# A two-layer graph network on one core: the stages between the layers reordered over four engines, and two waits of GpSimd moved

## The chip, the core and the metric

The kernel runs on one core of a Trainium2 chip. The metric is the device time of one execution in microseconds. The core has TensorE (PE, matrix products), VectorE (DVE), ScalarE (ACT), GpSimd (POOL, which here issues the indirect DMAs) and the queue of SyncE (SP), which issues the plain DMAs. Each engine works off its own queue in order and waits on semaphores.

## What is computed

6250 nodes with 128 features each, and 106250 directed edges sorted by target. Two layers, each with a layer norm and relu ahead of it and a residual behind it:

```python
h = maximum(layernorm(x), 0)
# layer 0: softmax aggregation, one weight for each edge and feature
msg = h[src] + edge_attr
m = segment_max(msg * beta, dst)
e = exp(msg * beta - m[dst])
agg = segment_sum(msg * e / segment_sum(e, dst)[dst], dst)
x = x + (agg @ H + bias + h)
h = maximum(layernorm(x), 0)
# layer 1: attention with 4 heads of 32
Wx = h @ W.T
e = leaky_relu(Wx[src] . a1 + Wx[dst] . a2, 0.2)
ex = exp(e - segment_max(e, dst)[dst])
x = x + elu(segment_sum(ex * Wx[src], dst) / segment_sum(ex, dst))
```

Everything is float32.

## The kernel before

**Groups.** In each layer the edges go by in 208 groups of 512 (NG), four blocks of 128. GpSimd fetches the source rows of a block with one indirect DMA (gather0, L658, into the ring ring_h of four groups; gather1, L689, into msg, a ring of eight). Ahead of a group it waits until its slot of the ring is free: in layer 0 until the group four back is lifted, in layer 1 until the products of the group eight back are made. Between the gathers of a group stands one more wait. In layer 0, ahead of the second gather, it is for the maxima of the group six back, turned back (unturned); in layer 1, ahead of the third, for the targets of the group four back.

**One group of layer 0.** ScalarE lifts the gathered rows into PSUM (lift0, L817), VectorE adds them to the edge's features (add0, L1141), TensorE turns the messages so that edges run along the free axis (turn0, L1395, semaphore msgT), VectorE scans them twice for the maxima of each target (maxima0, L1118 and L1123), TensorE turns the differences back (unturn0, L1401 and L1405), ScalarE makes the weights (weigh0, L799 and L803), VectorE the products (products0, L1153), TensorE sums both into a window of 512 targets with a one-hot matrix (segment_sums, L1386), and ScalarE merges the window into the accumulator acc (merge, L775 to L783). The stages of different groups overlap with fixed lags. Layer 1 does the like with narrow logits: the targets' logits (targets1, L1486), scans of 4 rows, unturn1 (L1504 and L1506), products1 (L1284).

**Between the layers** the 6250 nodes go by in 13 batches of 512 (NBAT; the last has 106). For each batch, in order:
- log0 and seed0 on ScalarE (L822, L827) make the reciprocal of the denominator from the accumulator; batch b can start when merge 196 + b is done.
- near0 on GpSimd multiplies it with both accumulators (L672 into nears(b), L674).
- lift_near0 on ScalarE copies nears(b) into PSUM (L836), quotient0 on VectorE corrects the quotient with it (L1177).
- layer_out on TensorE (L1438 the bias, L1443 the product). Its weights are every fourth column of the quotients, a step of 16 bytes.
- finish0 on VectorE adds the residual (L1183) and takes statistics (L969).

Only when all 13 are finished do the means follow (L1207, L1208), and then, again batch by batch, above1 on VectorE (subtract the mean and relu, L1216), turn_h (L1454), a copy out of PSUM (ScalarE L889 or VectorE L1242), layer_in (L1465) and the scaled copy of four tiles by ScalarE into msg (wx1, L899). The reciprocals of the spreads are made in between on VectorE by spreads1, 16 small operations (L1221 to L1231). SyncE stores each batch (L537, L539) to wx_dram, and gather1 waits for all of the stores.

The order on each engine is that of its program: ScalarE's tail of layer 0 interleaves weigh0, merge0, log0, seed0 and lift_near0 by hand; so does VectorE's with quotient0 and products0.

## Time and profile before

| | us |
|---|---|
| median of three runs (2255.95 to 2258.19) | 2258.1 |
| the profiled execution | 2257.1 |
| its span in the trace | 2255.3 |
| first gather of layer 0, from the start of the span | 37.96 |
| first gather of layer 1 | 1162.82 |

Times in the rows are microseconds from the start of the span, unless they are marked ns or stand in a column of mean ns. A row of the timeline gives the start, the duration, the engine, the line and what it writes and reads; equal neighbours are merged (x8), and the bracket tells how long the engine had stood idle before it and what ended that. "issue" is time in which an engine waited for nothing that the profile shows. PEld is TensorE's loading of weights, which runs beside its products.

### The profile page before, as it was taken

The page shows a single profiled execution, that of the slowest core. Times are in us where ns is not written, and L with a number is a line of the kernel's source. Part 1 is how long each engine was busy: PE and PEld are TensorE (multiplying, and loading weights), DVE is VectorE, ACT ScalarE, POOL GpSimd, SP SyncE. Part 2 cuts the span into 40 slices and gives each one's busy share as a digit, 9 for nine tenths or more (in the row PEclk, how much of TensorE's full clock was granted, in tenths as well). Part 3 has the DMA queues.
Part 4 walks back from the last instruction along what each step waited for, and adds up shares of the span by engine and source line. Part 5 has one row for each costly group of instructions (what it writes and reads, how often), then busy time and mean ns, then how long its engine had stood idle before and what let it go on. Part 6 is the DMA issues. An engine that isn't in the chain of part 4 may idle for free.

```text
span 2255.3 us, 62207 instructions
## 1 busy us (share of the span) xinstructions
PE 1935.5 (86%) x14541; PEld 1707.6 (76%) x14542; DVE 1986.2 (88%) x3873; ACT 1419.2 (63%) x3494; POOL 1645.6 (73%) x1739
## 2 busy tenths in 40 slices
PE   2888888888888888888969998989999999999996
PEld 1677777776776777777758888888888888888885
DVE  7999999999999999999759988888888888888886
ACT  3677777777677777777635555555555555555556
POOL 5777777777777777777627777777777777777775
PEclk9999999999999999999778999999999999999999
DMA  6444444444444444444023333333333333333331
GB/s 213 124 130 133 136 132 132 127 132 132 132 137 126 129 134 135 133 129 120 8 82 62 60 59 58 58 59 59 59 58 59 59 59 58 59 59 59 58 60 68
DMA packets 318697, 213.52 MB, mean 95 GB/s; under 512 B 169938, under 2 KB 279074, under 8 KB 318642
## 3 DMA queue, kind: packets, MB, share of 16 engines
q0 software_dynamic: 53184, 112.31, 20.9%
q1 hardware_dynamic: 264608, 100.15, 17.2%
q8 instruction: 23, 0.38, 0.1%
q10 hardware_dynamic: 850, 0.43, 0.1%
q14 instruction: 32, 0.26, 0.0%
HBM read 200.69 MB, written 10.29 MB: 94 GB/s over the span
## 4 chain that ended last, share of the span: by engine, by line
POOL 38%; issue 22%; DVE 13%; DMA 11%; PE 9%; ACT 3%; POOLq 1%; SPq 1%; DVEq 0%; ACTq 0%
POOL msg L689 25%; POOL ring_h L658 12%; DMA ring_h<-h_dram,meta_g 8%; DVE seg_max L1123 3%; DMA msg<-wx_dram,meta_g 3%; DVE sums L1118 2%; ACT banks L817 2%; PE sums L1405 2%; PE sums L1401 2%; DVE banks L1118 2%; DVE msg L1141 1%; PE banks L1395 1%; PE sums L1386 1%; PE sums L1443 1%; DVE onehot L1102 1%
## 5 line engine op out<-in xcount | busy, mean ns | idle before, releaser
L689 POOL DMA_INDIRECT msg<-wx_dram,meta_g x831 | 792.6, 954 | 299.1 <-issue 246.2
L658 POOL DMA_INDIRECT ring_h<-h_dram,meta_g x831 | 786.7, 947 | 266.2 <-issue 227.2
L1386 PE MATMUL sums<-onehot,prod 128*128 128x128 f32 x3296 | 685.7, 291 | 18.4 <-issue 6.5
L1386 PE MATMUL sums<-onehot,wgt 128*128 128x128 f32 x3296 | 669.0, 286 | 0.0
L1386 PEld LDWEIGHTS sums<-onehot,prod 128*128 128x128 f32 x3296 | 529.3, 202 | 52.7 <-issue 51.9
L1386 PEld LDWEIGHTS sums<-onehot,wgt 128*128 128x128 f32 x3296 | 532.1, 203 | 0.0
L783 ACT ACTIVATE acc<-sums 128x1022 f32 x410 | 419.9, 1024 | 0.1
L817 ACT ACTIVATE banks<-ring_h,sign 128x512 f32<-128x512 f32 x208 | 143.9, 692 | 269.9 <-DMA ring_h<-h_dram,meta_g 262.6
L1405 PEld LDWEIGHTS sums<-neg_ident,seg_max 128*128 128x128 f32 x1664 | 219.3, 192 | 100.0 <-issue 99.5
L1395 PE MATMUL banks<-ident,msg 128*128 128x128 f32 x832 | 136.7, 287 | 160.9 <-DVE msg L1141 160.9
L1118 DVE TENSOR_TENSOR_SCAN sums<-flags,seg_max,banks 4x512 f32<-4x512 bf16 x207 | 264.1, 1276 | 4.9 <-PE banks L1495 3.5
L1118 DVE TENSOR_TENSOR_SCAN banks<-flags,seg_max,banks 128x512 f32<-128x512 bf16 x207 | 264.8, 1279 | 0.0
L1123 DVE TENSOR_TENSOR_SCAN seg_max<-flags,banks 128x512 f32<-128x512 bf16 x208 | 253.9, 1220 | 7.2
L1123 DVE TENSOR_TENSOR_SCAN seg_max<-flags,sums 4x512 f32<-4x512 bf16 x208 | 251.2, 1208 | 7.2
L1395 PEld LDWEIGHTS banks<-ident,msg 128*128 128x128 f32 x832 | 88.3, 142 | 199.3 <-issue 183.5
L775 ACT ACTIVATE carried<-acc,scale 128x2 f32 x414 | 121.3, 293 | 164.2 <-PE sums L1386 147.2
L1486 PEld LDWEIGHTS banks<-window,onehotT 128*128 128x128 f32 x1664 | 213.7, 201 | 10.1 <-issue 8.9
L1405 PE MATMUL sums<-neg_ident,seg_max 128*128 128x128 f32 x1664 | 220.0, 275 | 0.0
L1141 DVE SCALAR_TENSOR_TENSOR msg<-msg,sign,banks 128x512 f32<-128x512 f32 x208 | 155.3, 746 | 72.1 <-ACT banks L817 66.7
L1401 PE MATMUL sums<-msg,ident 128*128 128x512 f32 x416 | 214.1, 597 | 2.3 <-ACT sums L803 2.2
L1486 PE MATMUL banks<-window,onehotT 128*128 128x4 f32 x1664 | 207.5, 248 | 9.1 <-DMA window<-wx_dram 8.7
L908 ACT ACTIVATE sums<-logit_d 128x16 f32<-128x16 f32 x208 | 39.1, 188 | 266.0 <-DVE logit_d L1276 263.2
(215 smaller groups left out, 2877.8 us busy)
## 6 DMA issues: line engine op xcount, KB each, us to landing
msg<-in_edge_attr SPq DMA_DIRECT2D x207, 256.0 KB, 3.2
flags<-flag_dram SPq DMA_DIRECT2D x52, 512.2 KB, 3.8
window<-wx_dram SPq DMA_DIRECT2D x832, 2.0 KB
ring_h<-h_dram,meta_g POOLq DMA_INDIRECT x831
msg<-wx_dram,meta_g POOLq DMA_INDIRECT x831
wx_dram<-msg SPq DMA_DIRECT2D x13, 272.0 KB, 2.1
nodes<-in_x SPq DMA_DIRECT2D x6, 512.0 KB, 7.1
h_dram<-acc SPq DMA_DIRECT2D x12, 256.0 KB
```

What stands on the lines that cost most here:

```text
L658: pool.indirect_dma_start(hg[0:n, s % HRING, b, :], None, h_dram, bass.IndirectOffsetOnAxis(ap=meta_g[0:n, s, b:b + 1], axis=0)).then_inc( ...
L689: pool.indirect_dma_start(msg[0:n, s, b, :], None, wx_dram, bass.IndirectOffsetOnAxis(ap=meta_g[0:n, s, b:b + 1], axis=0)).then_inc(L1["ga ...
L783: act.activation(acc[:, :, bass.ds(node + 1, WIN - 1)], where[:, :, 1:WIN], ACT.Copy).then_inc(k["merged"], 1)
L817: act.activation(row_psum, ring_h[:, s % HRING, :], ACT.Copy, scale=sign[:, 0:1]).then_inc(L0["lifted"], 1)
L1118: dve.tensor_tensor_scan(run, flag[:, 0:GE], data, before, ALU.add, ALU.max).then_inc(k["scanned"], 1)
L1123: dve.tensor_tensor_scan(seg_max[0:n, par, ::-1], flag[:, GE:0:-1], run[:, ::-1], -BIG, ALU.add, ALU.max).then_inc(k["scanned"], 1)
L1141: dve.scalar_tensor_tensor(msg[:, s, :, 0:D], msg[:, s, :, 0:D], sign[:, 0:1], row_psum.rearrange("p (b d) -> p b d", b=GB), ALU.mult, ALU.add
L1386: ins = pe.matmul(where[:, j, bass.ds(off, P)], what[:, slot, b, :], onehot[:, s, b, :], start=(b == 0), stop=(b == GB - 1), skip_group_ch ...
L1395: ins = pe.transpose(bank[s % 2][:, b * P:(b + 1) * P], msg[:, s, b, 0:D], ident[:, :])
L1401: pe.matmul(shift_psum.rearrange("p (b d) -> p b d", b=GB), ident[:, :], msg[:, s, :, 0:D], start=True, stop=False, skip_group_check=True)
L1405: ins = pe.matmul(shift_psum[:, b * P:(b + 1) * P], seg_max[:, s % 2, b * P:(b + 1) * P], neg_ident[:, :], start=False, stop=(b == GB - 1) ...
L1486: ins = pe.matmul(bank[1][:, b * H:(b + 1) * H], onehotT[:, s % 2, b * P:(b + 1) * P], window[:, s, b, :], start=True, stop=True)
```

## The change

**Waits of GpSimd in the layers.** In gather0, ahead of a group's second gather, the wait is now for the messages turned two groups back (msgT), from group 2 on. In gather1 it is ahead of the second gather, for the maxima turned back four groups back (unturned).

**End of layer 0.** lift_near0 leaves ScalarE. For batches 0 to 5 (LIFTS) TensorE does it as a product with the identity; from batch 6 on quotient0 reads nears(b) in SBUF. near0 has eight places (NEARS), four of them in ring_h. quotient0 writes its result tile by tile into msg (quot), reading its inputs with a step of four numbers, and layer_out's weights lie in one piece. layer_out(0) stands ahead of the last segment sums.

**Three parts.** Means are made for batches 0 to 5 once batch 5 is finished, for 6 to 9 behind batch 9, and for the rest at the end; the spreads of 0 to 5 behind batch 7, all others at the end. Subtracting the mean (less_mean) is now one operation for each batch, on GpSimd for eleven batches and on VectorE for 10 and 12, and the relu moves into the copy behind turn_h, on ScalarE except for batches 8 and 10. From layer_out(8) on TensorE puts turn_h and layer_in of the first batches in between. From batch 6 on VectorE scales the fourth tile (last_wx1). The stores of wx_dram are unrolled and wait for both engines.

The diff, cut to its core:

```diff
+        NEARS = 8
+        LIFTS = 6
+        EARLY = 6
+        MIDDLE = 10
+        QUOT = 4
+
         def nears(b):
-            return (diff[:, b % 2, :], hn_row[:, b % 2, :])[b // 2 % 2]
+            if b % NEARS < 4:
+                return (diff[:, b % 2, :], hn_row[:, b % 2, :])[b // 2 % 2]
+            return ring_h[:, b % 4, :]
...
-        HT_ACT = (0, 3, 6, 9, 12)
-        HT_DVE = tuple(b for b in range(NBAT) if b not in HT_ACT)
+        HT_DVE = (8, 10)
+        HT_ACT = tuple(b for b in range(NBAT) if b not in HT_DVE)
+        ABOVE_DVE = (10, 12)
+        ABOVE_POOL = tuple(b for b in range(NBAT) if b not in ABOVE_DVE)
+
+        def turn_bank(b):
+            if b < EARLY:
+                return (sums[:, 0, 0, :], bank[3])[b % 2]
+            return bank[b % 2]
 
         def wx_psum(b, t):
+            if b < EARLY:
+                return sums[:, 0, 1, 0:TW] if t == IN_BANK else bank[2][:, t * TW:(t + 1) * TW]
             return sums[:, b % 2, 1, 0:TW] if t == IN_BANK else bank[2 + b % 2][:, t * TW:(t + 1) * TW]
+
+        def tiles_of(b):
+            return range(1 if b == NBAT - 1 else GB)
+
+        def wx_by_dve(b, t):
+            return b >= EARLY and t == IN_BANK
+
+        WX_DVE = tuple(b for b in range(EARLY, NBAT - 1))
+
+        def wait_wx(eng, b):
+            eng.wait_ge(mid_wx, b + 1)
+            if b in WX_DVE:
+                eng.wait_ge(mid_wx_dve, WX_DVE.index(b) + 1)
 
         def wait_turned(eng, b):
             if b in HT_ACT:
                 eng.wait_ge(mid_hT_act, HT_ACT.index(b) + 1)
             else:
                 eng.wait_ge(mid_hT_dve, HT_DVE.index(b) + 1)
+
+        def less_mean(eng, b, done):
+            t = len(tiles_of(b))
+            lo = b * GB
+            eng.tensor_tensor(logs(b)[:, 0:t * D].rearrange("p (t d) -> p t d", d=D), nodes[:, lo:lo + t, :],
+                              norm[:, 1, lo:lo + t].rearrange("p (t a) -> p t a", a=1).to_broadcast([P, t, D]), ALU.add
+                              ).then_inc(done, 1)
...
-                    if b == 1 and later(g, 6):
-                        pool.wait_ge(L0["unturned"], g - 5)
+                    if b == 1 and later(g, 2):
+                        pool.wait_ge(L0["msgT"], g - 1)
...
-                if b >= 4:
-                    pool.wait_ge(mid_lifted, b - 3)
+                if b >= NEARS:
+                    pool.wait_ge(mid_lifted, b - NEARS + 1)
+                elif b >= 4:
+                    pool.wait_ge(L0["lifted"], NG - HRING + b % 4 + 1)
...
+            for b in ABOVE_POOL:
+                pool.wait_ge(mid_mean, 1 if b < EARLY else 2 if b < MIDDLE else 3)
+                less_mean(pool, b, mid_h_pool)
...
-                    if b == 2 and later(g, 4):
-                        pool.wait_ge(L1["targets"], g - 3)
+                    if b == 1 and later(g, 4):
+                        pool.wait_ge(L1["unturned"], g - 3)
...
-            def lift_near0(b):
-                w = LAST if b == NBAT - 1 else GE
-                act.wait_ge(mid_near, b + 1)
-                if b < 2:
-                    act.wait_ge(L0["scanned"], 2 * (NG - 1 + b))
-                else:
-                    act.wait_ge(mid_agg, b - 1)
-                act.activation(near_bank(b)[:, 0:w], nears(b)[:, 0:w], ACT.Copy).then_inc(mid_lifted, 1)
...
-                act.activation(hT[:, b % 2, 0:w], bank[b % 2][:, 0:w], ACT.Copy).then_inc(mid_hT_act, 1)
+                act.activation(hT[:, b % 2, 0:w], turn_bank(b)[:, 0:w], ACT.Relu).then_inc(mid_hT_act, 1)
...
-                if b == 0:
-                    act.wait_ge(normed, 3)
+                act.wait_ge(normed, 3 if b < EARLY else 4)
                 if b >= WXB:
                     act.wait_ge(wx_stored[b % WXB], 16 * (b // WXB))
-                for t in range(1 if b == NBAT - 1 else GB):
-                    n = b * GB + t
-                    ins = act.activation(msg[:, b % WXB, t, :], wx_psum(b, t), ACT.Copy, scale=norm[:, 0, n:n + 1])
+                for t in tiles_of(b):
+                    if not wx_by_dve(b, t):
+                        n = b * GB + t
+                        ins = act.activation(msg[:, b % WXB, t, :], wx_psum(b, t), ACT.Copy, scale=norm[:, 0, n:n + 1])
                 ins.then_inc(mid_wx, 1)
...
             def quotient0(b):
-                w = LAST if b == NBAT - 1 else GE
                 dve.wait_ge(mid_quot, b + 1)
-                dve.wait_ge(mid_lifted, b + 1)
-                rows = logs(b)[:, 0:w]
-                dve.scalar_tensor_tensor(rows, near_bank(b)[:, 0:w], 2.0, rows, ALU.subtract, ALU.mult).then_inc(mid_agg, 1)
+                if b < LIFTS:
+                    dve.wait_ge(mid_lifted, b + 1)
+                near = by_tile(near_bank(b) if b < LIFTS else nears(b), b)
+                dve.scalar_tensor_tensor(quot(b), near, 2.0, by_tile(logs(b), b), ALU.subtract, ALU.mult).then_inc(mid_agg, 1)
...
+            for b in range(NBAT):
+                if b + 1 < NBAT:
+                    quotient0(b + 1)
+                finish0(b)
+                if b == EARLY - 1:
+                    dve.wait_ge(measured, NBAT + EARLY)
+                    means(0, EARLY * GB)
+                if b == EARLY + 1:
+                    spreads(0, EARLY * GB)
+                if b == MIDDLE - 1:
+                    dve.wait_ge(measured, NBAT + MIDDLE)
+                    means(EARLY * GB, MIDDLE * GB)
+            dve.wait_ge(measured, 2 * NBAT)
+            means(MIDDLE * GB, NT)
+            dve.wait_ge(mid_mean, 3)
+
             def turned1(b):
...
+            less_mean(dve, 10, mid_h_dve)
+            less_mean(dve, 12, mid_h_dve)
+            spreads(EARLY * GB, NT)
+            last_wx1(6)
+            turned1(8)
+            last_wx1(7)
+            last_wx1(8)
+            turned1(10)
+            last_wx1(9)
+            last_wx1(10)
+            last_wx1(11)
+            dve.wait_ge(mid_wx_psum, NBAT)
...
+            def lift_near0(b):
+                pe.wait_ge(mid_near, b + 1)
+                if b < 2:
+                    pe.wait_ge(L0["scanned"], 2 * (NG - 1 + b))
+                else:
+                    pe.wait_ge(mid_agg, b - 1)
+                pe.matmul(near_bank(b), ident[:, :], nears(b), start=True, stop=True).then_inc(mid_lifted, 1)
...
-                    part = logs(b)[:, 0:LAST] if last else logs(b)[:, i:GE:GB]
-                    ins = pe.matmul(where[:, i * D:(i + 1) * D], part, phm_neg[:, :], start=False, stop=(i == t - 1),
+                    ins = pe.matmul(where[:, i * D:(i + 1) * D], quot(b)[:, i, :], phm_neg[:, :], start=False, stop=(i == t - 1),
...
+            last(unturn0, 1)
+            lift_near0(0)
+            pe.wait_ge(L0["onehots"], NG)
+            pe.wait_ge(L0["added"], NG)
+            last(sums0, 3, where=spare_sums0, free=1)
+            last(unturn0, 0)
+            lift_near0(1)
+            last(sums0, 2, free=1)
+            lift_near0(2)
+            last(sums0, 1, where=spare_sums0, free=1)
+            pe.wait_ge(phm_turned, 1)
+            pe.wait_ge(bias_split, 1)
+            pe.wait_ge(L0["weighed"], NG)
+            pe.wait_ge(L0["multiplied"], NG)
+            layer_out(0)
+            last(sums0, 0, free=1)
+            AHEAD_OUT = 8
+            for b in range(1, NBAT):
+                if b + 2 < LIFTS:
+                    lift_near0(b + 2)
+                layer_out(b)
+                if b >= AHEAD_OUT:
+                    if b == AHEAD_OUT:
+                        pe.wait_ge(L0["merged"], NG)
+                    turn_h(b - AHEAD_OUT)
+                    if b > AHEAD_OUT:
+                        layer_in(b - AHEAD_OUT - 1)
+            for b in range(NBAT - AHEAD_OUT, NBAT):
+                turn_h(b)
+                layer_in(b - 1)
+            layer_in(NBAT - 1)
             pe.wait_ge(mid_wx, NBAT)
 
 

```

## Rows read from the trace of the kernel before

**Rows 1.** The page, chain of waits that ended last, shares of the span by engine
```profile
POOL 38%; issue 22%; DVE 13%; DMA 11%; PE 9%; ACT 3%; POOLq 1%; SPq 1%; DVEq 0%; ACTq 0%
```

**Rows 2.** Waits of GpSimd, 200 to 1000 and 1200 to 2200: total, times, longest
```profile
POOL ring_h L658 <- issue: 174.7, 573, 0.3
...
POOL msg L689 <- issue: 235.8, 773, 0.3
```

**Rows 3.** Timeline, start of layer 0, GpSimd's first and tenth gather, TensorE's first turn
```profile
37.96 1.19 POOL L658 DMA_INDIRECT ring_h<-h_dram,meta_g  x1 [13.05 <-DMA h_dram<-acc]
...
49.81 0.95 POOL L658 DMA_INDIRECT ring_h<-h_dram,meta_g  x1 [0.30 <-issue]
...
54.23 1.09 PE L1395 MATMUL banks<-ident,msg 128*128 128x128 f32 x4 [2.64 <-DVE msg L1141]
```

**Rows 4.** Timeline: last gather of layer 0, a lift and the last merge, first gather after
```profile
1076.90 0.89 POOL L658 DMA_INDIRECT ring_h<-h_dram,meta_g  x1 [0.30 <-issue]
...
1094.25 0.62 ACT L836 ACTIVATE banks<-diff 128x512 f32<-128x512 f32 x1
...
1102.32 1.03 ACT L783 ACTIVATE acc<-sums 128x1022 f32 x1
...
1162.82 1.04 POOL L689 DMA_INDIRECT msg<-wx_dram,meta_g  x1 [45.95 <-DMA wx_dram<-msg]
```

**Rows 5.** Timeline, VectorE's residuals of batches 0, 1, 7 and 12
```profile
1102.86 0.69 DVE L1183 TENSOR_TENSOR nodes<-nodes,sums 128x512 f32<-128x512 f32 x1 [7.16 <-PE sums L1443]
...
1105.24 0.69 DVE L1183 TENSOR_TENSOR nodes<-nodes,sums 128x512 f32<-128x512 f32 x1
...
1121.02 0.69 DVE L1183 TENSOR_TENSOR nodes<-nodes,sums 128x512 f32<-128x512 f32 x1 [0.45 <-PE sums L1443]
...
1133.39 0.27 DVE L1183 TENSOR_TENSOR nodes<-nodes,sums 106x128 f32<-106x128 f32 x1
```

**Rows 6.** Timeline: two of the spreads' operations, first and last scaled copy by ScalarE
```profile
1136.17 0.24 DVE L1221 TENSOR_TENSOR newton<-stats 128x49 f32<-128x49 f32 x1
...
1136.45 0.21 DVE L1222 SCALAR_TENSOR_TENSOR norm<-newton 128x49 f32<-128x49 f32 x1
...
1140.18 0.91 ACT L899 ACTIVATE msg<-banks,norm 128x136 f32<-128x136 f32 x3 [2.90 <-DVE norm L1231]
...
1157.90 0.44 ACT L899 ACTIVATE msg<-banks,norm 128x136 f32<-128x136 f32 x1
```

**Rows 7.** Stretches: length, busy PE, PEld, DVE, ACT, POOL (count), clock, DMA, GB/s
```profile
1097.00:1133.00 36.00, 35.52 (x127) 27.86 (x127) 24.30 (x69) 13.74 (x30) 15.36 (x15) 0.61 0.00 1
1133.00:1159.00 26.00, 20.71 (x151) 18.81 (x151) 22.08 (x92) 16.10 (x54) 0.00 (x0) 0.89 0.31 119
```

**Rows 8.** Timeline near the end of layer 0: a turn, a second gather two groups later
```profile
1018.53 0.65 PE L1395 MATMUL banks<-ident,msg 128*128 128x128 f32 x4 [1.37 <-DVE msg L1141]
...
1020.60 0.95 POOL L658 DMA_INDIRECT ring_h<-h_dram,meta_g  x1 [0.31 <-issue]
```

**Rows 9.** TensorE: low-clock products; page row; layer_out's bias; weight loads, min/median/max ns
```profile
62.17 1.78 PE L1405 MATMUL sums<-neg_ident,seg_max 128*128 128x128 f32 x8
...
L1401 PE MATMUL sums<-msg,ident 128*128 128x512 f32 x416 | 214.1, 597 | 2.3 <-ACT sums L803 2.2
...
L1438 PE MATMUL sums<-bias_rows,ones_rows 3*128 3x512 bf16 x12 | 6.5, 543 | 0.1
...
L1443 PEld LDWEIGHTS sums<-phm_neg,elu_e x16: 309/329/332, 1105.6 to 1109.6; 128*128 128x128 f32 x16
...
L1465 PEld LDWEIGHTS banks<-w_aug,hT x74: 186/190/337, 1137.3 to 1157.2; 128*128 128x128 f32 x74
```

**Rows 10.** Timeline, layer 1: maxima of group 3 turned back, second gather of group 7
```profile
1195.74 0.39 PE L1506 MATMUL banks<-ident,seg_max 4*128 4x4 f32 x4
...
1199.19 0.94 POOL L689 DMA_INDIRECT msg<-wx_dram,meta_g  x1 [0.30 <-issue]
```

**Rows 11.** Timeline before layer 0: a sum on GpSimd, a VectorE operation beside it
```profile
22.11 1.26 POOL L636 TENSOR_TENSOR nodes<-nodes,acc 128x512 f32<-128x512 f32 x1 [0.27 <-ACT acc L738]
...
22.58 0.85 DVE L979 TENSOR_TENSOR newton<-stats 128x25 f32<-128x25 f32 x1
```

More of the change, by code:

```diff
@@ L875, in _ @@
             log0(12)
-            lift_near0(5)
             seed0(11)
             seed0(12)
-            for b in range(6, NBAT):
-                lift_near0(b)
             def turned1(b):
@@ L1199, in _, with means, spreads @@
             dve.wait_ge(pool_sum, len(POOL_SUMS))
-            for b in range(NBAT):
-                if b + 1 < NBAT:
-                    quotient0(b + 1)
-                finish0(b)
-            dve.wait_ge(measured, 2 * NBAT)
-            one, two = stats[:, :, 0:3], stats[:, :, 3:6]
-            link(dve.tensor_tensor(mean_2[:, :], one[:, :, 1], two[:, :, 1], ALU.add))
-            dve.tensor_scalar(norm[:, 1, :], mean_2[:, :], -0.5, None, ALU.mult).then_inc(mid_mean, 1)
-            dve.wait_ge(mid_mean, 1)
-            def above1(b):
-                if b >= 2:
-                    dve.wait_ge(mid_hT_psum, b - 1)
-                for t in range(1 if b == NBAT - 1 else GB):
-                    n = b * GB + t
-                    ins = dve.tensor_scalar(hn[:, b % 2, t, :], nodes[:, n, :], norm[:, 1, n:n + 1], 0.0, ALU.add, ALU.max)
-                ins.then_inc(mid_h, 1)
-            def spreads1():
-                y, t, v = norm[:, 0, :], newton[:, :], spread_v[:, :]
-                link(dve.tensor_tensor(t, one[:, :, 1], two[:, :, 1], ALU.subtract))
+            one, two = stats[:, :, 0:3], stats[:, :, 3:6]
+            def means(lo, hi):
+                link(dve.tensor_tensor(mean_2[:, lo:hi], one[:, lo:hi, 1], two[:, lo:hi, 1], ALU.add))
+                dve.tensor_scalar(norm[:, 1, lo:hi], mean_2[:, lo:hi], -0.5, None, ALU.mult).then_inc(mid_mean, 1)
+            def spreads(lo, hi):
+                y, t, v = norm[:, 0, lo:hi], newton[:, lo:hi], spread_v[:, lo:hi]
+                link(dve.tensor_tensor(t, one[:, lo:hi, 1], two[:, lo:hi, 1], ALU.subtract))
                 link(dve.scalar_tensor_tensor(y, t, 0.25, t, ALU.mult, ALU.mult))
-                link(dve.tensor_tensor(v, one[:, :, 2], two[:, :, 2], ALU.add))
+                link(dve.tensor_tensor(v, one[:, lo:hi, 2], two[:, lo:hi, 2], ALU.add))
                 link(dve.scalar_tensor_tensor(v, v, 1.0 / D, y, ALU.mult, ALU.add))
@@ L1234, in spreads1, with last_wx1 @@
                 ins.then_inc(normed, 1)
+            for b in range(NBAT):
+                if b + 1 < NBAT:
[12 more added lines that the diff above has]
+            dve.wait_ge(mid_mean, 3)
             def turned1(b):
[L1237 to L1238 removed]
                 dve.wait_ge(mid_hT_psum, b + 1)
[L1240 to L1250 removed]
+                dve.wait_ge(mid_wx_psum, b - 1)
+                dve.tensor_scalar(hT[:, b % 2, :], turn_bank(b), 0.0, None, ALU.max).then_inc(mid_hT_dve, 1)
+            def last_wx1(b):
+                dve.wait_ge(mid_wx_psum, b + 1)
+                if b == WX_DVE[0]:
+                    dve.wait_ge(normed, 4)
+                dve.wait_ge(wx_stored[b % WXB], 16 * (b // WXB))
+                n = b * GB + IN_BANK
+                dve.tensor_scalar(msg[:, b % WXB, IN_BANK, :], wx_psum(b, IN_BANK), norm[:, 0, n:n + 1], None, ALU.mult
+                                  ).then_inc(mid_wx_dve, 1)
+            less_mean(dve, 10, mid_h_dve)
[10 more added lines that the diff above has]
+            dve.wait_ge(mid_wx_psum, NBAT)
             def one_hot1(g, s, use):
@@ L1412, in _ @@
             pe.wait_ge(beta_ready, 1)
-            sweep_edges(pe, [(4, sums0), (0, turn0), (2, unturn0)], until=NG - 1)
-            last(unturn0, 2)
-            last(turn0, 0)
-            last(sums0, 4)
-            last(unturn0, 1)
-            pe.wait_ge(L0["onehots"], NG)
-            pe.wait_ge(L0["added"], NG)
-            last(sums0, 3, where=spare_sums0, free=1)
-            last(unturn0, 0)
-            last(sums0, 2, free=1)
-            last(sums0, 1, where=spare_sums0, free=1)
-            last(sums0, 0, free=1)
-            pe.wait_ge(phm_turned, 1)
-            pe.wait_ge(bias_split, 1)
+            def lift_near0(b):
[5 more added lines that the diff above has]
+                pe.matmul(near_bank(b), ident[:, :], nears(b), start=True, stop=True).then_inc(mid_lifted, 1)
             def layer_out(b):
-                last = b == NBAT - 1
-                t, rows = (1, LAST) if last else (GB, P)
+                t, rows = extent(b)
                 if b >= 2:
@@ L1459, in layer_in @@
                 wait_turned(pe, b)
-                if b >= 2:
-                    pe.wait_ge(mid_wx, b - 1)
-                elif b == 0:
+                back = 1 if b <= EARLY else 2
+                if b >= back:
+                    wait_wx(pe, b - back)
+                if b == EARLY + 1:
                     pe.wait_ge(self_res, NBAT)
-                for t in range(1 if b == NBAT - 1 else GB):
+                for t in tiles_of(b):
                     ins = pe.matmul(wx_psum(b, t), hT[:, b % 2, t * P:(t + 1) * P], w1_aug[:, :], start=True, stop=True)
                 ins.then_inc(mid_wx_psum, 1)
-            straight(NBAT, [(0, turn_h), (1, layer_in)])
+            sweep_edges(pe, [(4, sums0), (0, turn0), (2, unturn0)], until=NG - 1)
+            last(unturn0, 2)
+            last(turn0, 0)
+            last(sums0, 4)
+            last(unturn0, 1)
[29 more added lines that the diff above has]
+            layer_in(NBAT - 1)
             pe.wait_ge(mid_wx, NBAT)
```

51 lines of the change are left out of this document (24 added, 27 removed).

## Prediction

> **What bounds the kernel now.** I read the chain of waits first. It puts most of the span on GpSimd, whose only large work is to issue the gathers: 831 for each layer [rows 1]. The list of waits then shows that GpSimd waits for nothing during a layer. Before nearly every gather there is the same 0.3 us of its own, and nothing longer [rows 2]. So a layer lasts as long as its gathers: the first of layer 0 starts at 37.96, the last at 1076.90 [rows 3, 4], and 1038.94 / 830 is 1.25 us a gather, 5.0 us a group of four. The rest of the span is what lies before the first gather, between the last of layer 0 and the first of layer 1 (1076.90 to 1162.82, [rows 4]), and behind the last. The two layers change only if GpSimd is made to wait. The middle changes with whatever sets its pace, which differs from part to part.
>
> **The middle before.** It has four parts. (a) The last groups are worked off until the last merge ends at 1102.32 + 1.03 = 1103.35; ScalarE is the full engine there. (b) Thirteen batches go through quotient, layer_out, residual and statistics. VectorE alone would need 2.38 us a batch (1102.86 to 1105.24), but later it waits 0.45 us for TensorE in each, and the residuals of batches 1 to 12 span 1105.24 to 1133.39 + 0.27 = 1133.66, that is 28.4 us [rows 5]. (c) Means and the first layer_in work lead to the first scaled row block at 1140.18. (d) Thirteen batches of layer_in follow at 1.45 us, the last one ending at 1157.90 + 0.44 = 1158.34 [rows 6], and the store and one wait lead to 1162.82. Between 1097 and 1133 TensorE is busy nearly throughout at a mean granted clock of 0.61 of 2.4 GHz, so at the lower level of 1.2 for most of it [rows 7].
>
> **GpSimd's wait in layer 0.** The wait asks for the turn of the group two back, from group 2 on. In the steady part it costs nothing. A row near the end shows the tightest case there: the turn starts at 1018.53 and takes 0.65; the second gather of the group two later is at 1020.60, and the gather before it ends at 1020.30, so 1.1 us are in hand [rows 8]. At the start it does cost. The second gather of group 2 is the tenth gather, at 49.81; the turn of group 0 starts at 54.23 and ends at 55.32, as its messages were added only then [rows 3]. GpSimd must stand for 5.5 us and a semaphore's delay, 5.6 in all. Before, GpSimd used that time to run ahead, and kept the lead until the last gather. With the others following at a fixed distance, everything behind is 5.6 later. The queue behind the wait is only GpSimd's own gathers; ScalarE's lift waits for them. Bounds: 5.0 (the others start with less backlog) to 8 (TensorE turns the next groups at the lower clock, at which eight loads with their products take 1.78 us [rows 9], and holds GpSimd once more). **+5.6.**
>
> **GpSimd's wait in layer 1.** The turned-back maxima of group 3 are done at 1195.74 + 0.39 = 1196.13; the second gather of group 7 is at 1199.19, the one before it ends at 1198.88 [rows 10]. That leaves 2.7 us early in the layer, where TensorE is slowest. **0**, bounds 0 to 1. The indices and rows of the lists don't change.
>
> **(a) lifts from ScalarE to TensorE.** Four copies of 0.62 us, such as the one at 1094.25, stand in ScalarE's queue before the last merge [rows 4], spaced by 0.52, so 2.1 us leave it. But three of them now stand in TensorE's queue among the last sums and turns, each two passes of 0.6 us that overlap to 0.9 [rows 9], and the first layer_out goes ahead of the last sum. I take the merge 0.6 us earlier. The gain is larger for the residual of batch 1, as layer_out 0 is done already: about 1103.2 instead of 1105.24, **-2.0**; bounds -3 and 0.
>
> **(b) the loop of thirteen.** VectorE's 2.38 us a batch become the limit if TensorE is in time: layer_out's weights are now read in one piece, and such a load takes 190 ns where the strided one takes 329 [rows 9]. Eleven steps of 2.38 less 0.5 for the short batch are 25.7. Into the same queue come two means of 0.5 (0.24 + 0.21 and gaps) and 16 operations of 0.21 to 0.24 with gaps, 3.7 us, which are half of the spreads [rows 6]: 30.4. The quotients now read the near values and the logarithms with a step of four numbers. No row has a long VectorE operation read so. The nearest is 0.24 against 0.21 for 49 numbers with a step of six [rows 6], which bounds it by 0 and 0.35 us a quotient; as other parts hide some, I take 0.15 for eleven, 1.7. The last term is waiting, 2.5 us, from the next two paragraphs. Sum 34.6 against 28.4: **+6.2**, bounds +2 and +10.
>
> A cost that the edit brings: less_mean puts eleven operations with two SBUF inputs on GpSimd, 1.26 us each by the nearest row, while VectorE runs quotients from batch 6 on (now with both inputs in SBUF) and the spreads. The trace shows what such a meeting does: at 22.58 a VectorE operation on 128x25 numbers takes 0.85 us, and ends at 23.43, just as GpSimd's sum from 22.11 is over at 23.37; of the same kind alone, 128x49 take 0.24 [rows 6, 11]. Four or five such meetings at up to 1.2 us are 3 to 5 us on VectorE; part of it lies where VectorE would wait for TensorE anyway. The Trainium skill's page "SBUF — State Buffer" (Who interferes with whom) states this as a rule: a VectorE instruction with two SBUF inputs and a GpSimd one that reads SBUF block each other for the whole instruction. By that rule the trace agrees, and it speaks against where this change puts the sums.
>
> TensorE's clock decides the rest of the waiting. At the lower clock a batch of layer_out takes about 1.78 and 0.5 for the bias, 2.3 [rows 9], which just fits beside 2.38; together with a turn (1.1, as that of group 0 in [rows 3]) and a layer_in (eight products of 136 columns, so about 1.9) it is 5.3 and does not. I assume that the lower clock comes as before, and that the denser work from batch 8 on ends it within some microseconds.
>
> **(c), (d) what is left after the loop.** Before, from the last residual to the last row block: 1158.34 - 1133.66 = 24.7. Now: statistics 0.3, means 0.5, two less_means 1.0, the other half of the spreads 3.7 and a meeting 0.5: 6.0. Then batches 6 to 12 of layer_in (0 to 5 are done beside the loop) at 1.45, with the small one, 10.3; ScalarE's fourth tile and TensorE's 1.45 are both within that. Sum 16.3, **-8.4**; bounds -9 and -4. Relu in place of Copy, the unrolled stores and the bias change nothing; the store behind the last batch is as before.
>
> Middle: -2.0 + 6.2 - 8.4 = -4.2. With the start: +1.4. The profiled run took 2257.1 us (span 2255.3), the median of the other three is 2258.1; made against the profiled one the sum is 2258.5.
>
> **Rivals.** First, the clock stays low for longer, as it did before until near 1139. Then batches 8 to 12 of the loop run at TensorE's 5.3 us with turns and layer_ins in them instead of 2.6, and the middle gains nothing: 2257.1 + 5.6 + 0.3 = 2263.0. It decides from about 8 us of lower clock behind batch 8 on; if the clock never came back in the middle, thirteen layer_ins at about 3 instead of 1.45 would add 20 more, 2283. For it speaks the 0.61 [rows 7], against it that the work is denser than before. This one ends slower. 0.22.
>
> Second, the middle pays as designed: no meetings, no price of the step, full clock. Then (b) is +2.0 and the middle -8.4 to -9, giving 2253.5. Against it stands the row at 22.58 [rows 11]. 0.15.
>
> Third, the change's wait does not do what it says at the start: GpSimd isn't held, as the turn of group 0 comes earlier or the lead is won back. 2258.5 - 5.6 = 2252.9. Nothing before the first turn is changed, so I see no way: 0.08.
>
> Fourth, the wait holds GpSimd in the steady part too, because 1.1 us is little: 0.1 us in each of 206 groups would be 20 us, 2279. Every delay of GpSimd widens its margin, which speaks against it. 0.05.
>
> **How the numbers follow.** My case has 0.50, at 2258.5, with 2254.5 to 2262.5 by its bounds. The range reaches into both sides, 2251 to 2266. About 0.2% is what a measurement of this kernel can tell from no change, 4.5 us, so faster is below 2253.6 and slower above 2262.6. Faster: the third, most of the second, 0.02 of mine: 0.20. Slower: 0.16 of the first, the fourth, 0.02 of mine: 0.23. The rest, 0.57, is no change.
>
> **What would show it.** Right: a gap of 5 to 6 us before GpSimd's tenth gather and none later; the last gather of layer 0 near 1082.5; from there to the first of layer 1 about 82 us instead of 85.9; VectorE's small spreads of 0.8 to 1.2 us beside GpSimd's sums; 1039 to 1046 us of gathers in layer 1. Wrong: a middle below 77 or above 87 us, further gaps among the gathers, or a lead at the end of layer 0 as before.

## The result, and the profile after

The changed kernel takes 2270.6 us (median of 4 runs, 2268.1 to 2271.3), the kernel before 2257.2 beside it (4 runs): a ratio of 1.0057, 95% interval 1.0045 to 1.0069, so 13.5 us slower. The profiled run took 2268.1 us, with a span of 2266.3 for 2255.3, which is 11.0 more. Those 11 us are what the two traces have to explain.

The chain of waits of the changed kernel, shares of the span by engine (before in [rows 1]), and GpSimd's waits from 40 to 1092 us (total, times, longest; before in [rows 2]):

```profile
POOL 40%; issue 34%; PE 9%; DVE 7%; DMA 6%; ACT 2%; POOLq 1%; SPq 1%; ACTq 0%; DVEq 0%
...
POOL ring_h L708 <- issue: 249.2, 790, 2.3
POOL ring_h L708 <- PE banks L1447: 15.1, 30, 6.2
```

GpSimd still sets the pace, but its longest wait in layer 0 is no longer 0.3 us. There is one of 6.2 for a turn of TensorE (L1447), and, filed under "issue", some of up to 2.3. GpSimd's timeline shows both kinds (start, length, what it is, idle before it and what ended that), with the last gather of layer 0 and the first of layer 1, which answer to [rows 3, 4]:

```profile
54.81 0.94 POOL L708 DMA_INDIRECT ring_h<-h_dram,meta_g  x1 [6.24 <-PE banks L1447]
...
183.62 0.95 POOL L708 DMA_INDIRECT ring_h<-h_dram,meta_g  x1 [0.30 <-PE banks L1447]
186.85 0.95 POOL L708 DMA_INDIRECT ring_h<-h_dram,meta_g  x1 [2.28 <-issue]
188.11 0.94 POOL L708 DMA_INDIRECT ring_h<-h_dram,meta_g  x1 [0.30 <-issue]
...
1090.08 0.88 POOL L708 DMA_INDIRECT ring_h<-h_dram,meta_g  x1 [0.30 <-issue]
...
1173.60 1.04 POOL L745 DMA_INDIRECT msg<-wx_dram,meta_g  x1 [19.04 <-DMA wx_dram<-msg]
```

The tenth gather starts 7.2 us after the ninth, where the usual distance is 1.25: 5.9 lost. The 114th starts at 186.85, 3.2 us after its forerunner, and the same is found at every 104th gather from there, seven times (distances 3.23, 1.98, 2.31, 2.44, 2.74, 2.01 and 2.32 us): 17.0 less 7 times 1.25 is 8.3 lost. Layer 0 goes from 37.00 to 1090.08, which is 1053.1 for 1038.9.

| From the traces, us | before | after | difference |
|---|---|---|---|
| First gather of layer 0 | 37.96 | 37.00 | -1.0 |
| Layer 0, first to last gather | 1038.9 | 1053.1 | +14.1 |
| Middle, last gather to first of layer 1 | 85.9 | 83.5 | -2.4 |
| Layer 1, first to last gather | 1044.9 | 1044.7 | -0.2 |
| From the last gather on | 47.6 | 48.0 | +0.4 |

The first line is no effect of the change: over all traces, below too, that gather starts between 37.0 and 38.5, with either kernel.

What happens at the seven late gathers is seen at the first of them, in the chain of waits (start, length, what; the record of POOLq at L48 is the moment in which GpSimd's queue has passed the wait ahead of the second gather):

```profile
182.90 0.67 PE banks L1447 x4
...
183.59 0.02 POOLq L48
...
184.57 2.28 issue
186.85 0.75 POOL ring_h L708
```

The turn ends, the queue passes the wait at 183.59, and the gather that it holds starts at 186.85, 3.25 us later. All times of GpSimd's queue below are read from such records in the traces.

In most of the experiments the kernel before took 3024 to 3037 us beside the kernel tried (one and the same chip gave 2252 us in one run and 3037 in a later one), TensorE's granted clock in the layers was about 0.88 and 0.76 instead of 1.00 and 0.94, and GpSimd waited for other engines in most groups, so their whole times are compared with the kernel before beside them alone, and only their queue's pauses and the batch loop of the middle are read against the 2257 us of this section.

### The profile page after: what moved, and what is told of

Read it like the earlier page. It is cut to its first block, busy times and chain, and to the rows that moved or that the text cites. A ratio compares the mean times of both kernels' runs of the same rounds, so it can differ in the third digit from the quotient of the medians.

```text
span 2266.3 us, 62179 instructions
## 1 busy us (share of the span) xinstructions
PE 1934.2 (85%) x14553; PEld 1703.1 (75%) x14554; DVE 1988.0 (88%) x3846; ACT 1414.8 (62%) x3481; POOL 1659.3 (73%) x1750
## 3 DMA queue, kind: packets, MB, share of 16 engines
q1 hardware_dynamic: 264608, 100.15, 17.1%
## 4 chain that ended last, share of the span: by engine, by line
POOL 40%; issue 34%; PE 9%; DVE 7%; DMA 6%; ACT 2%; POOLq 1%; SPq 1%; ACTq 0%; DVEq 0%
POOL ring_h L708 21%; POOL msg L745 19%; DMA ring_h<-h_dram,meta_g 4%; PE sums L1438 3%; DVE sums L1157 1%; DVE seg_max L1162 1%; DMA msg<-wx_dram,meta_g 1%; ACT banks L873 1%; DVE msg L1180 1%; PE banks L1447 1%; PE banks L1564 1%; PE banks L1573 1%; PE banks L1582 1%; PE banks L1555 0%; PE banks L1509 0%
## 5 line engine op out<-in xcount | busy, mean ns | idle before, releaser
L1447 PE MATMUL banks<-ident,msg 128*128 128x128 f32 x832 | 137.3, 288 | 170.5 <-DVE msg L1180 170.0
L1447 PEld LDWEIGHTS banks<-ident,msg 128*128 128x128 f32 x832 | 88.9, 142 | 208.9 <-issue 187.1
```

The costliest lines, as they stand in the source:

```text
L1447: ins = pe.transpose(bank[s % 2][:, b * P:(b + 1) * P], msg[:, s, b, 0:D], ident[:, :])
```

## Experiments

**The old wait of layer 0 put back into the changed kernel**, and **the new one put alone into the kernel before**.

```diff
-                    if b == 1 and later(g, 2):
-                        pool.wait_ge(L0["msgT"], g - 1)
+                    if b == 1 and later(g, 6):
+                        pool.wait_ge(L0["unturned"], g - 5)
```

> The changed kernel with layer 0's old wait for GpSimd (turned-back maxima of the group six back, from group 6 on). Theory A (the new wait takes GpSimd's lead away, so that the 5.9 us at the start and seven pauses of GpSimd's own queue, some 8.3 us in all, come onto the path): no gap among the gathers of layer 0, about 14 us less than the changed kernel, some 2256 us; the middle stays at 83.5. Rival B (the pauses belong to the changed program as a whole, its place in memory or its longer body, and not to the wait): the seven gaps stay, and only the 5.9 us at the start go, about 2264 us.

> The kernel before with nothing but layer 0's new wait. Theory A: the same gaps as in the changed kernel, 5.9 us before the tenth gather and 2.0 to 3.2 before every 104th from the 114th on, so about 14 us more than before, 2271 us. Rival B: only the gap at the start, about 2263 us.

Measured, with the kernel before at 3034.3 us: 3045.6 with the old wait (ratio 1.0036, interval 1.0021 to 1.0051), and 2979.6 with the new one (0.9816, 0.9784 to 0.9849). Neither theory had this. In this condition the new wait is worth 1.8%: layer 0 takes 1366 us, where the kernel before with its old wait there takes 1410 (in the run on layer 1 below); GpSimd is held by others anyway. The same pair once more gave 3025.9 and 2962.9 against 3023.8 (0.9998 and 0.9789). I did not find out what the new wait does better there.

The pair still says something of the pause. With the old wait, the gap stands at the 114th gather all the same, as in this condition the queue has no lead with that wait either: it passes it 0.7 us before the gather, in the median (GpSimd's timeline, changed kernel with the old wait, second run):

```profile
220.60 0.94 POOL L708 DMA_INDIRECT ring_h<-h_dram,meta_g  x1 [0.30 <-issue]
225.83 0.95 POOL L708 DMA_INDIRECT ring_h<-h_dram,meta_g  x1 [4.28 <-issue]
```

In the first run with the old wait, the records of GpSimd's queue have the same thing at the 114th, 218th, 322nd and so on, seven times: a wait is passed, and 3.23 to 3.24 us later the gather behind it starts, where other groups need 0.7. In the changed kernel it is 3.23 to 3.24 at the same seven gathers. So the pause belongs to GpSimd's queue, whichever wait stands there. It is in the trace of the kernel before, too: at the same seven groups its queue takes 3.9 to 4.1 us from one wait to the next, where the others take 1.4 to 2.2 and some up to 2.8. But there the queue passes the wait 9.8 to 10.8 us ahead of the gather, and the pause is over before a gather needs it.

**The new wait alone, where the kernel before takes 2254 us:**

> The kernel before with nothing but layer 0's new wait, once more, as the runs so far fell on chips where the kernel before takes 3030 us and other things set the pace of a layer. Where it takes 2257: theory A (the wait takes GpSimd's lead, and a pause of its queue of 3.25 us at every 104th gather, which is in all traces so far, comes onto the path) gives 1053 us from the first to the last gather of layer 0 instead of 1039 and 2271 us in all, 0.6% slower. Rival B (the loss needs the changed program) gives 2263 us at most.

Measured: 2267.0 us against 2254.2, a ratio of 1.0058, interval 1.0042 to 1.0075. One moved wait loses as much as the whole change, 1.0057. So the whole times show nothing of the 2.4 us that the table gives the middle, which is less than the 3.2 us by which four executions of the changed kernel differ. Its gathers:

```profile
55.77 0.94 POOL L658 DMA_INDIRECT ring_h<-h_dram,meta_g  x1 [6.53 <-PE banks L1395]
...
184.34 0.94 POOL L658 DMA_INDIRECT ring_h<-h_dram,meta_g  x1 [0.30 <-PE banks L1395]
187.53 0.95 POOL L658 DMA_INDIRECT ring_h<-h_dram,meta_g  x1 [2.24 <-issue]
```

The start loses 6.5 us and the seven pauses 8.4. Layer 0 takes 1051.5 us, 12.6 more than in [rows 3, 4], as a gather was a little shorter throughout that run (layer 1 has 1042.5 for 1044.9). Rival B, which wanted the changed program for the later gaps, is out.

**The wait only from group 8 on** (the changed kernel with `later(g, 8)` in place of `later(g, 2)`).

> The changed kernel with layer 0's new wait only from group 8 on. Theory A (two separate costs: a stall of the start and the pauses of the queue): the gap before the tenth gather goes, the pauses before the 114th and every 104th after it stay, as by then GpSimd has no lead again; where a gather takes 1.25 us this is some 6 us less than the changed kernel. Rival B (only the start costs, the later gaps follow from it): the later gaps go too.

One run each: 2265.2 us, the kernel before 2252.3. The gathers are as theory A says:

```profile
49.48 0.94 POOL L708 DMA_INDIRECT ring_h<-h_dram,meta_g  x1 [0.30 <-DMA meta_g<-meta]
...
181.34 0.95 POOL L708 DMA_INDIRECT ring_h<-h_dram,meta_g  x1 [1.90 <-issue]
...
1084.85 0.88 POOL L708 DMA_INDIRECT ring_h<-h_dram,meta_g  x1 [0.30 <-issue]
```

The stall of the start is gone and the seven pauses are there (8.1 us). Layer 0 takes 1047.2 us, 8.3 more than before and 5.9 less than with the change, so the two costs are separate and add up. The whole time fell by 2.9 only, as in that run the first gather was 0.6 later, layer 1 1.2 longer and the end 1.8 longer. Against the one run of the kernel before beside it, it is 12.9 us slower, hardly less than the change: the 5.9 us are shown by the gathers, not by the whole time.

**One group further back** (the changed kernel with `later(g, 3)` and msgT of g - 2).

> The changed kernel with layer 0's wait on messages turned three groups back instead of two, from group 3 on. Theory A: the lead is about a group (5 us) longer, which covers the 3.25 us that the queue takes at every 26th group, so no gaps in the steady part; at the start GpSimd waits for the turn of group 0 before the 14th gather instead of the tenth, so about 1 us is left of the 5.9. Some 2257 us. Rival B: the seven gaps stay at 2.0 to 3.2 us, about 2265 us.

2992.1 us against 3034.3 (0.9863, interval 0.9830 to 0.9896), and 2986.4 against 3034.1 when repeated. GpSimd waited in nearly every group for reasons of its own, so whether a group more of lead hides the pause where GpSimd sets the pace was not measured. An estimate from the changed kernel's trace: the lead there is 2.1 us in the median, and a group is 5.0, so 7.1 us of lead against 3.25.

**The new wait of layer 1 alone, in the kernel before.**

```diff
-                    if b == 2 and later(g, 4):
-                        pool.wait_ge(L1["targets"], g - 3)
+                    if b == 1 and later(g, 4):
+                        pool.wait_ge(L1["unturned"], g - 3)
```

> The kernel before with nothing but layer 1's new wait. Theory A: GpSimd keeps more than 3.3 us of lead in layer 1, so nothing changes, 2257 us, and the gathers of layer 1 take 1044.9 us as before. Rival: the wait costs there what it costs in layer 0 as soon as the lead is short, 8 us of gaps more, 2265 us.

3043.5 us against 3034.3 (1.0030, interval 1.0015 to 1.0046): 9 us slower in the other condition, which proves nothing for this one. Here the changed kernel itself answers: 1044.7 us of gathers in layer 1 for 1044.9, and 1045.9 in the run from group 8 on. The prediction's 0, with bounds 0 to 1, held.

This layer also tests the explanation by the lead. In the changed kernel's layer 1 the queue takes 3.66 to 3.74 us from the new wait to the next at nine groups, those of the 114th gather and of every 88th after it, where all others take 2.0 at most: a pause is there too. But the queue passes the wait 4.7 to 6.3 us ahead of the gather at these nine, and no gather of the layer is late. So a pause of 2.9 us (its length is read in the next runs) costs nothing with that lead, and one of 3.25 us costs 8.3 with 2.1 us in layer 0.

**What the pause counts.** Two runs, one execution each. In the first, half of the rows are left out of each gather of layer 0 in groups 8 to 199 (the messages of the other half are missing). In the second, six idle instructions stand behind the wait.

> The changed kernel, where in layer 0 the gathers from group 8 on fetch 64 rows each instead of 128 (half of the messages are left out, so the output is another). It asks what GpSimd's queue counts between two pauses. If it counts rows or their descriptors, the pauses come every 208 gathers from there on; if it counts gathers or instructions, every 104 as before (114th, 218th, 322nd and so on). Theory: descriptors, so 208.

> The changed kernel with six more instructions that do nothing behind layer 0's new wait in each group, in GpSimd's queue alone. If the pause comes after so many instructions or bytes of the program, it comes more often than every 26 groups; if it counts descriptors or gathers, it stays at every 104 gathers. Theory: stays at 104.

2977.0 and 2981.5 us, the kernel before at 3029.9. With 64 rows the extra gap comes every 116 gathers (the 245th, 361st, 477th and so on), neither 104 nor 208, so the expectation was wrong; such a gather still takes 0.90 us instead of 0.95. With the idle instructions it stays at 104, but they left no record in the trace, and from the wait to the gather it is 0.71 and 3.25 us as without them, so this run says little. Two readings of the traces add to it. In the first run with the old wait, layer 1, whose rows have 544 bytes instead of 512, has pauses of 2.9 us every 88 gathers (the 114th, 202nd, up to the 818th; one of them):

```profile
1740.28 0.94 POOL L745 DMA_INDIRECT msg<-wx_dram,meta_g  x1 [4.23 <-issue]
```

And on the DMA queues that carry instructions no packet lies between 173 and 1058 us of the changed kernel's trace, while the seven pauses lie between 183 and 974 us, so nothing that these queues carry explains them. Nor does the program's own loop, whose body is 8 groups, 32 gathers: 104 is no multiple of it. The spacing follows what a gather fetches (88, 104, 116), but far from in proportion. What is counted stays open.

**The price of the quotient's step.** All three of the next have the old wait of layer 0. The first reads the quotients' inputs in one piece and writes with a step. The second also subtracts the means of batches 0 to 5 on ScalarE.

```diff
-                near = by_tile(near_bank(b) if b < LIFTS else nears(b), b)
-                dve.scalar_tensor_tensor(quot(b), near, 2.0, by_tile(logs(b), b), ALU.subtract, ALU.mult).then_inc(mid_agg, 1)
+                w = LAST if b == NBAT - 1 else GE
+                near = near_bank(b) if b < LIFTS else nears(b)
+                k = 1 if b == NBAT - 1 else GB
+                ins = (v[:, 0:w].rearrange("d (p t) -> d p t", t=k) for v in (near, logs(b)))
+                dve.scalar_tensor_tensor(quot(b).rearrange("d t p -> d p t"), next(ins), 2.0, next(ins), ALU.subtract, ALU.mult
+                                         ).then_inc(mid_agg, 1)
...
+            for b in ABOVE_ACT:
+                for t in tiles_of(b):
+                    n = b * GB + t
+                    ins = act.activation(logs(b)[:, t * D:(t + 1) * D], nodes[:, n, :], ACT.Identity, bias=norm[:, 1, n:n + 1])
+                ins.then_inc(mid_h_act, 1)
```

> The changed kernel with the old wait of layer 0, and the quotients read in one piece and written tile by tile (numbers 544 bytes apart), where the change reads with a step of four numbers and writes in one piece; TensorE's weights stay in one piece. Theory: it is the strided reading of two inputs that costs 0.38 us each (1.07 against 0.69); written with a step a quotient takes 0.7 to 0.75 us and the middle is 3 us shorter than with the old wait alone, 80.5 us, about 2251 us. Rival: any step in any operand costs the same, or VectorE isn't the limit in these steps: 1.07 and no gain, 2254 us.

> As the one before, and the means of batches 0 to 5 are subtracted on ScalarE (24 activations with a bias) instead of on GpSimd, so that no GpSimd operation stands beside VectorE's quotients and first spreads. Theory: the three stretched spreads (0.45, 0.95, 0.98 us) go back to 0.18 each and the stretched quotient from 1.34, 2 us of VectorE's time in all, and the middle is 2 us shorter again, about 2249 us; the 24 activations take 6 to 7 us in which ScalarE is idle now. Rival: TensorE at its lower clock is the limit there (8 products in 2.07 us), and the time moves by less than 1 us.

What can be compared is the loop of thirteen, from the residual of batch 1 to the end of that of batch 12, which takes 35.8 to 36.4 us in six runs of the changed kernel with the old wait, 35.8 with the change, and 35.2 to 36.1 in the other five runs whose loop is the same; nearly all of that spread is in one step, from batch 9 to 10, where VectorE waits for TensorE. The first edit gives 34.8 us. A quotient takes 1.01 to 1.07 us, so its record is nearly as long with a step in the output as with steps in the inputs, and the theory's 0.7 to 0.75 was wrong. But where VectorE works without a break (batches 1 to 2, 3 to 4 and 4 to 5) the distance of two residuals falls from 2.53-2.57 us to 2.42-2.46, against 2.38 without any step. The second gives 34.0. In whole times nothing can be told: 0.9998 (0.9985 to 1.0011) and 0.9993 (0.9982 to 1.0004) of the kernel before, at 3024 us. VectorE's first spreads in the second one:

```profile
1494.22 0.18 DVE L1260 TENSOR_TENSOR newton<-stats 128x24 f32<-128x24 f32 x1
1494.44 0.18 DVE L1261 SCALAR_TENSOR_TENSOR norm<-newton 128x24 f32<-128x24 f32 x1
1494.65 0.20 DVE L1262 TENSOR_TENSOR spread_v<-stats 128x24 f32<-128x24 f32 x1
```

Without GpSimd's sums beside them they take 0.18 to 0.20 us (the change: 0.45, 0.95 and 0.98, below). The step of the loop that holds them is 5.81 us instead of 7.34; TensorE took 0.7 of the 1.5 back by being later for batch 10 (4.29 for 3.59).

The third edit has the quotients contiguous on both sides, and layer_out's weights read with a step of four, as before the change.

> The changed kernel with layer 0's old wait, the means of batches 0 to 5 subtracted on ScalarE, and the quotients read and written in one piece, with TensorE's weights of layer_out read with a step of four numbers as before the change. Theory: a quotient takes 0.68 us again, 0.38 less, and the loop of thirteen, 34.0 us with the other two edits, loses 2 to 4 us: less than 12 times 0.38, as TensorE's eight products take 2.1 instead of 1.16 us at the full clock and become the limit in part. Rival: TensorE takes it all back, 34 us or more. In the whole time, where before takes 2257: 2251 us by the theory, 2253 by the rival.

The rival held: the loop takes 36.15 us, 2.2 more than in the run above, and the whole 3045.5 against 3036.6 (1.0027, interval 1.0012 to 1.0042). TensorE and VectorE in its loop:

```profile
1489.16 0.69 DVE L1236 TENSOR_TENSOR nodes<-nodes,sums 128x512 f32<-128x512 f32 x1 [2.77 <-PE sums L1499]
...
1492.40 0.69 DVE L1236 TENSOR_TENSOR nodes<-nodes,sums 128x512 f32<-128x512 f32 x1 [0.98 <-PE sums L1499]
...
1493.47 2.13 PE L1499 MATMUL sums<-phm_neg,msg 128*128 128x128 f32 x8
...
1497.23 0.67 DVE L1229 SCALAR_TENSOR_TENSOR msg<-banks,fin 128x512 f32<-128x512 f32 x1
...
1498.02 0.69 DVE L1236 TENSOR_TENSOR nodes<-nodes,sums 128x512 f32<-128x512 f32 x1
```

The quotient is at 0.67 us, but eight products with strided weights take 2.13 us (1.16 in the change at the same clock), and VectorE waits for them. Of the three ways tried to arrange the quotients, the step is better on VectorE than in TensorE's weights.

**The middle in the whole time.** The changed kernel with the old wait again, four times, with this expectation:

> The changed kernel with layer 0's old wait, where the kernel before takes 2257 us: no gap among the gathers of layer 0 (1038.9 us), the middle at 83 us against 86, so 2 to 3 us less than before, 2254 us, within 0.2% of it. Rival: without the wait GpSimd comes with more in hand to the end of layer 0 and the middle gets longer by that, so no gain at all, 2257 us.

Each time the kernel before took 3034 to 3037 us: ratios of 1.0025, 1.0034, 1.0014 and 1.0025 (intervals of 0.0011 to 0.0016 to either side). So in that condition this version is 0.1 to 0.4% slower than the kernel before in five of six runs, and the same in one (0.9998). The 2254 us that the traces suggest for it where the kernel before takes 2257, 2268 less 14, are an estimate; they were not measured.

## Why the prediction was wrong, point by point

**The failed step is layer 0's wait in the steady part.** The text says that it costs nothing there, by a margin of 1.1 us between the end of the turn and the end of the gather ahead, 1.4 us to the second gather itself [rows 8]. That margin was read off the gathers alone. The term left out is the way of GpSimd's queue from the passed wait to the gather: 0.7 us at least, and 3.25 us once in 26 groups. With the old wait the queue was some 10 us ahead and both were hidden. With the new one the turn holds it: the queue passes the wait 0.04 us behind the end of the turn in 205 of 206 groups, and the gather follows 0.7 to 3.8 us later, 2.1 in the median. That covers the usual 0.7 but not 3.25; seven times, 8.3 us.

The trace of the kernel before had both numbers. From the end of the turn to the second gather two groups later it has 1.67, 2.44, 2.24, 1.95, 1.77, 2.63 and 2.25 us at the seven groups at which its queue pauses, 14.95 in all; 7 times 3.29 (0.04 and 3.25) less 14.95 is 8.1 us, and 8.3 were measured. The fourth rival (0.05) had the place right, the wait holding GpSimd in the steady part, but its mechanism, a little in each of 206 groups, and its price of 20 us were wrong: seven groups carry the loss.

**The start was right**: 5.6 us forecast, 5.9 measured, before the tenth gather. It is one turn waited for, and [rows 3] held it. Within it two sizes were off against each other: from the passed wait to the gather it is 0.71 us and not 0.1 (54.10 to 54.81), while the turn of group 0 ended 5.2 us after the time at which the gather was due (54.06 for 48.88), and not 5.5.

**Layer 1's wait**: 0 forecast, -0.2 measured, in part by luck. The margin of 2.7 us, 3.1 to the gather [rows 10], hardly covers that layer's pause of 2.9; by the first pause the lead had grown to 4.7.

**The lifts, part (a)**: -2.0 forecast. The residual of batch 1 starts at 1116.30, 26.2 us after the last gather, for 28.3: -2.1.

**The loop, part (b)**: +6.2 forecast, +7.4 measured (35.8 for 28.4). Its rows, VectorE in the changed kernel:

```profile
1116.30 0.69 DVE L1222 TENSOR_TENSOR nodes<-nodes,sums 128x512 f32<-128x512 f32 x1 [1.41 <-PE sums L1484]
...
1121.64 0.69 DVE L1222 TENSOR_TENSOR nodes<-nodes,sums 128x512 f32<-128x512 f32 x1
...
1123.22 1.03 DVE L1216 SCALAR_TENSOR_TENSOR msg<-banks,fin 128x512 f32<-128x512 f32 x1
1124.17 0.68 DVE L1222 TENSOR_TENSOR nodes<-nodes,sums 128x512 f32<-128x512 f32 x1
...
1134.17 0.45 DVE L1247 TENSOR_TENSOR newton<-stats 128x24 f32<-128x24 f32 x1
1134.65 0.95 DVE L1248 SCALAR_TENSOR_TENSOR norm<-newton 128x24 f32<-128x24 f32 x1
1135.63 0.98 DVE L1249 TENSOR_TENSOR spread_v<-stats 128x24 f32<-128x24 f32 x1
1136.65 0.18 DVE L1250 SCALAR_TENSOR_TENSOR spread_v<-spread_v,norm 128x24 f32<-128x24 f32 x1
...
1147.11 0.69 DVE L1222 TENSOR_TENSOR nodes<-nodes,sums 128x512 f32<-128x512 f32 x1 [0.82 <-PE sums L1484]
...
1151.83 0.29 DVE L1222 TENSOR_TENSOR nodes<-nodes,sums 106x128 f32<-106x128 f32 x1 [0.29 <-PE sums L1484]
```

- The step of the quotient: the record is 0.38 us longer (1.03 to 1.11 for 0.67 to 0.69), but the distance of two residuals grows only from 2.38 to 2.53 (1121.64 to 1124.17), since a record begins before the one ahead of it ends. So 0.15 each, the forecast's value. The length of a record is not its price.
- Meetings with GpSimd and waiting for TensorE: 2.5 forecast in one term, about 3.7 measured. The three stretched spreads cost 1.8, and VectorE stood 0.2, 0.8, 0.55 and 0.3 for layer_out in the last batches, 1.9. This term is the one mis-sized. GpSimd's side of the meeting:

```profile
1131.69 2.87 POOL L415 TENSOR_TENSOR elu_e<-nodes,norm 128x512 f32<-128x512 f32 x2
1134.52 2.04 POOL L415 TENSOR_TENSOR fin<-nodes,norm 128x512 f32<-128x512 f32 x2
```

- The spreads without stretching took 3.4 instead of 3.7, as 24 numbers take 0.18 each and not 0.21.

The Trainium skill's page "SBUF — State Buffer" (Who interferes with whom) was cited for VectorE and GpSimd blocking each other; here the trace agrees again, with 0.95 beside 0.18 for the same operation; the first and the third stretched spread end at 1134.62 and 1136.61, each 0.05 to 0.06 us behind the end of a pair of GpSimd's sums (1134.56 and 1136.56).

**Parts (c) and (d)**: -8.4 forecast, -7.5 measured (17.1 for 24.7). From the last residual to the last spread it is 6.0 us, as forecast. But of layer_in the batches 0 to 2 alone were done at the last residual, not 0 to 5. Batches 0 to 6 share one set of banks, and from batch 3 on TensorE waits for ScalarE's copies before each:

```profile
1160.11 0.93 PE L1509 MATMUL banks<-w_aug,hT 128*128 128x136 f32 x6 [0.91 <-ACT msg L938]
```

At 2.5 us a batch the first scaled block of batch 6 came at 1161.31, 3.2 after its factor was there.

**TensorE's clock** (stretches of the changed kernel, columns as in [rows 7]):

```profile
1116.00:1152.00 36.00, 28.75 (x144) 21.96 (x142) 31.92 (x86) 8.15 (x22) 18.70 (x17) 0.72 0.04 16
1152.00:1170.00 18.00, 13.86 (x110) 12.41 (x107) 10.49 (x38) 12.66 (x40) 1.55 (x1) 1.00 0.38 144
```

The first rival, the clock staying low for longer, did not come: the mean is 0.72 in the loop and 1.00 behind it, for 0.61 and 0.89 in [rows 7]. The granted clock is at its lower level from 1124.9 to 1145.4, 20.5 us, for 30.7 before (1108.2 to 1138.9); it comes back 5 us behind the residual of batch 8, less than the 8 us that the rival needed. The second, a middle that pays as designed, failed on the meetings and the single banks; its own sum gives 2253.7 to 2254.3 and not 2253.5, so it lies in "no change". The third, GpSimd not held at the start, was wrong.

The middle as a whole: -4.2 forecast, -2.4 measured. Sum: -1.0 + 14.1 - 2.4 - 0.2 + 0.4 = 10.9 of the 11.0 us. Without the pauses it would have been 2.7, and without the earlier first gather, which is no effect of the change, 3.7, for 1.4 forecast; the rest is nearly all the middle's 1.8.

## What to carry to other kernels

Where an engine's queue runs ahead of the engine, its lead is a buffer, and a wait for a later event takes it away even if that event always comes before the engine needs it. Before moving such a wait nearer, ask for the longest the queue ever takes from a wait to the next issue, not the usual one, and look for it in the queue's own records at points where the engine shows nothing. The price of a changed operation is the distance between its neighbours' starts, not the length of its record.

## What the runs showed of the hardware

- GpSimd's queue pauses for 2.2 to 2.5 us beyond its usual 0.7 at a fixed spacing of indirect gathers: every 104 with 128 rows of 512 bytes (3.25 us from the wait to the gather), every 88 with rows of 544 (2.9). With 64 rows of 512 bytes gathers are late every 116. The pause delays a gather only where the queue's lead is shorter: by 0.7 to 2.0 us with leads around 2.1, not at all with 4.7 to 6.3 or with 10.
- A gather of 64 rows takes 0.90 us, one of 128 rows 0.95.
- A VectorE operation on 128x512 with a step in an input takes 1.03 to 1.11 us, with a step in the output 1.01 to 1.07, and with neither 0.67; between neighbours the first costs 0.15 to 0.19 and the second 0.04 to 0.08.
- Eight 128x128 products take 2.13 us at the full clock with weights at a step of 16 bytes and 1.16 with contiguous ones.
- One and the same wait makes the kernel 0.6% slower where it takes 2254 us and GpSimd is the limit, and 1.8 to 2.1% faster where it takes 3024 to 3034. Why was not found.
